# Removing the 22 filler products of TensorE from the first sequence of a fused mLSTM and ternary-FFN kernel

## The chip, the cores and the metric

The kernel runs on one core of one Trainium2 chip. The metric is device time in microseconds (us) of one execution; several executions are timed and the median is given. One execution is also recorded by the hardware profiler, and all rows below come from that one.

## The reference, cut to what matters

The input x has 16 independent sequences of 512 tokens by 512 features, in float32. Each goes through an mLSTM block and a feed-forward block, both with a layer norm ahead and a residual behind:

```python
x = x + mlstm(layernorm(x), Wq, Wk, Wv, Wog, Wig, big, Wfg, bfg, gamma, Wout)
w1_q, w2_q = ternary(w1), ternary(w2)        # sign(w) where |w| >= 0.7 * mean|w|, else 0
x = x + gelu(layernorm(x) @ w1_q.T + b1) @ w2_q.T + b2
```

The mLSTM has 8 heads and, step by step, a decaying state; the kernel computes it in four chunks of 128 tokens (scores within a chunk, a state between chunks), divides by a norm, normalises each head, multiplies by a sigmoid gate and projects with Wout. The ternary weights w1 (2048 by 512) and w2 (512 by 2048) have to be made from float32 weights once, before the first feed-forward block can start.

## The kernel before, in words

One program works through the 16 sequences. In its order the mLSTM of sequence b lies beside the feed-forward block of sequence b - 1: TensorE's list (the function `sequence` of the tensor block) mixes the products of both. Five engines each have one fixed list of instructions, written out by hand, and meet at semaphores.

The first sequence, b = 0, has no feed-forward block of an earlier sequence beside it. Its `sequence(0, None, True)` instead contains the one-time work on weights. `outer(b)` is followed by `first_heads()` (line 2155), which the change touches. The names needed to follow it:

- `scores(0, g)` (products at line 1913) makes the scores of four heads; VectorE multiplies them by the decay (`weigh`, line 1426), and GpSimd zeroes what lies in the future (`earlier_only`, line 661).
- `chunk_heads(j)` makes the output of chunk j, 8 heads, with the float32 products of line 1950 (two records each, so 16 per chunk); at j = 1 it first issues the 48 small products of line 1939 with the states of the chunks before.
- `head_stats` on VectorE (lines 1446 to 1514) reads the result of a chunk and computes its norms. It is followed on VectorE by the other chunks' `head_stats`, in order.
- `ternary_transpose(q)` (line 1789) is 8 transposes of 128 by 128 in float16, of pair q of blocks of w1 or w2, into bank q % 2 of the PSUM tile `pf`. It waits for `small_gone(q)` on VectorE (line 1213), which divides the weights by the threshold, and for `ternary_out(q - 2)` on ScalarE (line 832), which takes the sign and so frees the bank.
- `weights_out` transposes Wout (line 1756, float32); ScalarE and VectorE split it into two float16 parts (`weights_hi`, line 793; `weights_lo`, line 1192). `weights_ready(*USES_OUT)` waits for the last of these splits, and `project(0, t)` (12 products, line 1871) needs them.
- `keep_busy(bank, times)` is the filler: it issues `times` products of 128x128 by 128x512 in float16 (identity times a piece of `wT`) into a bank of `pf`. Nobody reads their result; a transpose overwrites the bank. `busy_until(q, times)` waits until bank q % 2 is free, issues the filler there and then calls `ternary_transpose(q)`.

In `first_heads()` the filler stands at three places: 6 products ahead of `ternary_transpose(5)`, 8 ahead of `ternary_transpose(9)`, and 8 in bank 0 ahead of `weights_ready(*USES_OUT)` and the first projection. TensorE's clock is granted at one of two levels, and the profile shows the granted share: 1.00 is 2.4 GHz and 0.50 is 1.2 GHz.

Of the kernel before, what the change touches and what calls it, by code (L numbers as in the profile page):

```python
# [46 lines left out]
HI, LO = 0, 1  # L47
# [24 lines left out]
def block_program(nc, x, Wq, Wk, Wv, Wog, Wig, big, Wfg, bfg, gamma, Wout, w1, b1, w2, b2, out):  # L72
    B, S, D = x.shape
# [47 lines left out]
    with ExitStack() as ctx:  # L121
        def sb(name, shape, dt=F32):
            return ctx.enter_context(nc.sbuf_tensor(name, shape, dt))

        def pb(name):
            return ctx.enter_context(nc.psum_tensor(name, [P, 2, 512], F32))

        def sem(name):
            return ctx.enter_context(nc.semaphore(name))


        wT = sb("wT", [P, 2, KD, 4 * D], F16)
# [8 lines left out]
        ident16 = sb("ident16", [P, P], F16)  # L141
# [70 lines left out]
        pa, pf = pb("pa"), pb("pf")  # L212
# [42 lines left out]
        pf_free = [sem("pf_free0"), sem("pf_free1")]  # L255
# [99 lines left out]
        def tok(t):  # L355
            return slice(t * P, (t + 1) * P)
# [78 lines left out]
        def pair_halves(q):  # L435

            return (x2T[:, :, :, :, :].rearrange("p a t k c -> p (a t k c)")
                    .rearrange("p (n u d) -> p n u d", n=4, u=2)[:, q % 4, :, :])

        def pair_bank(q):  # L440
            return pf[:, q % 2, :].bitcast(F16).rearrange("p (u k c) -> p u k c", u=2, c=P)
# [1296 lines left out]
        def _(pe):  # L1738
# [39 lines left out]
            def weights_ready(*uses):  # L1778
                for n in uses:
                    pe.wait_ge(s_wfree[w_bank(n)], w_taken(n) + 1)  # L1780

            def ternary_transpose(q):

                pe.wait_ge(s_small_gone, q + 1)
                if q >= 2:
                    pe.wait_ge(pf_free[q % 2], q // 2)
                for i in range(2):
                    for k in range(KD):
                        last = nc.tensor.transpose(pair_bank(q)[:, i, k, :], pair_halves(q)[:, i, tok(k)], ident16[:, :])
                last.then_inc(s_ufill, 1)  # L1790

            def keep_busy(bank, times):

                for _ in range(times):
                    nc.tensor.matmul(bank, ident16[:, :], wT[:, HI, 0, 0:D], start=True, stop=True)

            def take_pa(b, use):

                count = pa_taken(b, use)
                if not (isinstance(count, int) and count == 0):  # L1800
                    pe.wait_ge(pa_free[pa_bank(b, use)], count)
                return pa[:, pa_bank(b, use), :]
# [21 lines left out]
            def x_ready(b):  # L1824

                if b == 0:
                    for n in range(2):
                        pe.wait_ge(pa_free[n], KD // 2)
                elif b == 1:
                    pe.wait_ge(x1T_loaded, 32)  # L1830
                else:
                    pe.wait_ge(xT_loaded, at(b, 16, -16))

            def gates(b):
                bank = take_pa(b, U_GATE)
                for n, (ws, xs) in enumerate(PARTS):
                    for k in range(KD):
                        last = nc.tensor.matmul(bank[k * QUAD:(k + 1) * QUAD, :], wgT[:, k, ws, :], xT[:, xs, :, k, :],  # L1838
                                                start=(n == 0), stop=(n == 2), skip_group_check=True)
                last.then_inc(pa_fill, 1)  # L1840
# [10 lines left out]
            def tokens(b, use, src, col):  # L1851

                token_products(take_pa(b, use), src, col).then_inc(pa_fill, 1)

            def late_values(b, t):

                if not (isinstance(b, int) and b == 0):
                    pe.wait_ge(ph_free, at(b, PH_USES, 0))
                if t == 1:
                    if not (isinstance(b, int) and b == 0):  # L1860
                        pe.wait_ge(ps_free[1], at(b, PS_USES[1], 0))
                    bank, fill = ps[:, 1, :], ps_fill
                else:
                    bank, fill = ph[:, t - 2, :], ph_fill
                token_products(bank, xT[:, :, t, :, :], C_V).then_inc(fill, 1)
# [33 lines left out]
            def scores(b, g):  # L1899

                heads_of = range(g * H4, (g + 1) * H4)
                for n in heads_of:
                    if not in_ps(n):
                        take_pa(b, score_use(n))
                    elif n > 0 or not (isinstance(b, int) and b == 0):
                        pe.wait_ge(ps_free[n % 2], ps_done(b, n) - 1)
                if g == 0:
                    pe.wait_ge(kq_split, at(b, 2, 2))
                for j in range(T):
                    for i, (ks, qs) in enumerate(PARTS):  # L1910
                        for h, n in enumerate(heads_of):
                            rows_of = slice(h * DQ, (h + 1) * DQ)
                            last = nc.tensor.matmul(score_bank(n)[:, tok(j)], k_halves[rows_of, ks, g, tok(j)],  # L1913
                                                    q_halves[rows_of, qs, g, tok(j)], start=(i == 0), stop=(i == 2))
                            if j == T - 1 and i == 2 and h > 0:
                                last.then_inc(ps_fill if in_ps(n) else pa_fill, 1)
# [48 lines left out]
            def project(b, t):  # L1965
                pe.wait_ge(hoT_loaded[t], at(b, 16, 16))
                tokens(b, U_Y + t, hoT[:, t, :, :, :], C_OUT)
# [60 lines left out]
            def sequence(b, fb, ahead):  # L2028
# [63 lines left out]
                if first:  # L2092
                    first_heads()
                    return
# [39 lines left out]
                late_values(b, 1)  # L2134
                tokens(b, U_V, xT[:, :, 0, :, :], C_V)

            def busy_until(q, times):

                pe.wait_ge(pf_free[q % 2], q // 2)
                keep_busy(pf[:, q % 2, :], times)  # L2140
                ternary_transpose(q)

            def chunk_heads(j):

                chunk_state(0, j)
                for h in range(NH):
                    chunk_head(0, j, h)

            def weights_out(*ks):

                for k in ks:
                    pe.wait_ge(pa_free[k % 2], pa_done(0, U_H0 + k % 2))
                weights(*(USES_OUT[k] for k in ks))

            def first_heads():

                scores(0, 0)
                ternary_transpose(2)
                ternary_transpose(3)
                scores(0, 1)  # L2160
                ternary_transpose(4)
                busy_until(5, 6)
                chunk_heads(0)
                ternary_transpose(6)
                chunk_heads(1)
                ternary_transpose(7)
                weights_out(0, 1)
                chunk_heads(2)
                chunk_heads(3)
                ternary_transpose(8)  # L2170
                weights_out(2, 3)
                busy_until(9, 8)
                pe.wait_ge(pf_free[0], 5)
                keep_busy(pf[:, 0, :], 8)
                weights_ready(*USES_OUT)
                project(0, 0)
                ternary_transpose(10)
                ternary_transpose(11)
                project(0, 1)
                ternary_transpose(12)  # L2180
                ternary_transpose(13)
                ternary_transpose(14)
                x_ready(1)
                gates(1)
                ternary_transpose(15)
                late_values(1, 1)
                tokens(1, U_V, xT[:, :, 0, :, :], C_V)
                project(0, 2)
                project(0, 3)
# [44 lines left out]
```

## Time and profile before

| what | value |
|---|---|
| median of 3 executions | 1758.36 us (1758.11 to 1758.88) |
| the profiled execution: its own time | 1758.34 us |
| the profiled execution: span from first to last instruction | 1756.6 us |
| mean granted clock of TensorE | 0.992 |
| TensorE (PE) busy | 1710.4 us, 97% |
| VectorE (DVE) busy | 1445.4 us, 82% |
| ScalarE (ACT) busy | 1051.5 us, 60% |
| GpSimd (POOL) busy | 606.7 us, 35% |

All times in rows count from the span's start. PE stands for TensorE's products, PEld for its loads of the stationary operand, SP for the queue of the DMA issues. A row of a timeline merges neighbouring instructions of one kind: its length runs from the first one's start to the last one's end. In brackets stands how long the engine had been idle and what released it. The chain of work that ended last is followed back from the last instruction to whatever released each step.

### The profile page before, as it was taken

Reading aid. Unit: us, or ns where it says so; the run is one execution under the profiler, and the core shown is the slowest. Engines: PE = TensorE matmul, PEld = TensorE weight load, DVE = VectorE, ACT = ScalarE, POOL = GpSimd, SP = SyncE. Lnnn points to the kernel's source line nnn. Section 1 sums busy time; section 2 is a strip of 40 time slices with the busy share of each in tenths; the row PEclk is TensorE's granted clock in tenths of the full one; section 3 lists DMA queues with packets and bytes.
Section 4 is the critical chain, followed back from the end, with each engine's and each line's share of the span. In section 5 each row is a group of like instructions: output and inputs, shape, how many; then the busy total and the mean of one; then the engine's idle time right before and its main releaser. Section 6 shows DMA issues by size and latency. Waiting matters only on the chain.

```text
span 1756.6 us, 31370 instructions
## 1 busy us (share of the span) xinstructions
PE 1710.4 (97%) x12026; PEld 842.8 (48%) x12026; DVE 1445.4 (82%) x2536; ACT 1051.5 (60%) x1761; POOL 606.7 (35%) x477
## 2 busy tenths in 40 slices
PE   5789999999999999999999999999999999999999
PEld 3454444444454444445444444444445444454455
DVE  6778979888897978889887897988789797886872
ACT  5857557383764837466483755738376483746643
POOL 1142423525143352414425242342514335241440
PEclk8899999999999999999999999999999999999999
DMA  8736243272534526253362724426253452624120
GB/s 294 216 95 158 59 126 97 55 176 60 133 83 104 130 55 167 59 128 86 90 153 53 163 59 121 103 55 177 60 137 78 100 135 55 142 63 131 33 55 25
DMA packets 294981, 187.45 MB, mean 107 GB/s; under 512 B 239136, under 2 KB 260640, under 8 KB 289712
## 3 DMA queue, kind: packets, MB, share of 16 engines
q1 hardware_dynamic: 293248, 182.30, 40.9%
q10 hardware_dynamic: 1584, 3.15, 0.5%
q8 instruction: 95, 1.56, 0.4%
q14 instruction: 54, 0.44, 0.1%
HBM read 96.47 MB, written 20.23 MB: 66 GB/s over the span
## 4 chain that ended last, share of the span: by engine, by line
PE 85%; DVE 8%; DMA 2%; issue 2%; SPq 1%; ACT 1%; POOL 1%; POOLq 0%; DVEq 0%; ACTq 0%
PE pf L2018 24%; PE pf L2002 22%; PE pa L1871 19%; PE pa L1847 7%; PE psh L1871 6%; PE psh L1958 2%; SPq L530 1%; DMA kT<-shared 1%; PE psh L1913 1%; PE psh L1992 1%; PE pa L1838 1%; PE pa L1958 1%; PE psh L1954 1%; DVE gT L1577 1%; PE psh L1894 1%
## 5 line engine op out<-in xcount | busy, mean ns | idle before, releaser
L2018 PE MATMUL pf<-w2T,gT 128*128 128x512 f16 x2048 | 505.9, 379 | 0.0
L2002 PE MATMUL pf<-x2T,w1T 128*128 128x512 f16 x1920 | 422.0, 379 | 0.0
L2002 PEld LDWEIGHTS pf<-x2T,w1T 128*128 128x128 f16 x1920 | 185.3, 98 | 222.7
L2018 PEld LDWEIGHTS pf<-w2T,gT 128*128 128x128 f16 x2048 | 195.4, 97 | 177.5 <-DVE ktok L1456 0.5
L1577 DVE SCALAR_TENSOR_TENSOR gT<-g,wscale,gT 128x512 f16<-128x512 f32 x240 | 209.8, 878 | 20.2 <-ACT gT L986 18.1
L1871 PE MATMUL pa<-wT,xT 128*128 128x512 f16 x960 | 213.0, 379 | 1.9 <-ACT sig L910 1.9
L983 ACT ACTIVATE g<-pf,b1c 128x512 f32<-128x512 f32 x240 | 164.0, 683 | 72.5 <-PE pf L2002 58.0
L1871 PE MATMUL pa<-wT,shared 128*128 128x512 f16 x768 | 177.5, 381 | 4.5 <-DVE wT L1192 3.7
L986 ACT ACTIVATE gT<-g,wscale 128x512 f16<-128x512 f32 x240 | 173.3, 722 | 7.8
L1847 PE MATMUL pa<-xT,wT 128*128 128x512 f16 x768 | 171.8, 380 | 0.9 <-ACT kT L928 0.8
L991 ACT ACTIVATE ktok<-kT 128x512 f32<-128x512 f32 x64 | 40.4, 631 | 217.5 <-DVE kT L1472 217.5
L950 ACT ACTIVATE dec<-dec,gtok 128x128 f32<-128x128 f32 x512 | 154.5, 394 | 0.0
L1871 PEld LDWEIGHTS pa<-wT,xT 128*128 128x128 f16 x960 | 94.0, 98 | 114.7 <-ACT sig L910 2.0
L679 POOL TENSOR_TENSOR dec<-dec 128x1024 f16<-128x1024 f32 x30 | 72.0, 2398 | 200.1 <-ACT dec L1001 200.1
L1871 PE MATMUL psh<-wT,xT 128*128 128x512 f16 x576 | 129.5, 379 | 0.0
L700 POOL TENSOR_TENSOR x1b<-xres,b2r 128x512 f32<-128x512 f32 x64 | 80.6, 1268 | 132.6 <-DVE xres L1534 128.9
L684 POOL TENSOR_TENSOR hinv<-hvar,half 128x8 f32<-128x8 f32 x64 | 105.2, 1644 | 49.8 <-DVE hvar L1514 49.8
L1871 PEld LDWEIGHTS pa<-wT,shared 128*128 128x128 f16 x768 | 75.0, 98 | 96.7 <-DVE wT L1192 4.2
L691 POOL TENSOR_TENSOR qT<-kT,qT 128x512 f16<-128x512 f32 x64 | 74.4, 1163 | 132.7 <-ACT qT L1010 132.7
L661 POOL TENSOR_SCALAR_AFFINE_SELECT dec<-dec 128x1024 f32<-128x1024 f32 x64 | 92.1, 1439 | 72.4 <-DVE dec L1426 72.2
L1847 PEld LDWEIGHTS pa<-xT,wT 128*128 128x128 f16 x768 | 74.6, 98 | 87.9 <-ACT kT L928 0.9
L651 POOL TENSOR_TENSOR rstd<-ve,half 128x4 f32<-128x4 f32 x16 | 16.1, 1008 | 277.9 <-DVE ve L1238 277.9
(243 smaller groups left out, 2704.4 us busy)
## 6 DMA issues: line engine op xcount, KB each, us to landing
dec<-gate_r SPq DMA_DIRECT2D x32, 1024.0 KB, 5.8
xin<-L_attn_x SPq DMA_DIRECT2D x16, 1024.0 KB, 6.0
out<-x1b SPq DMA_DIRECT2D x64, 256.0 KB, 2.2
xres<-L_attn_x SPq DMA_DIRECT2D x16, 512.0 KB, 4.1
xres<-L_attn_x SPq DMA_DIRECT2D x32, 256.0 KB, 3.0
qw<-gate_w SPq DMA_DIRECT2D x128, 48.0 KB, 2.0
s<-state_w SPq DMA_DIRECT2D x60, 97.5 KB, 2.3
qw<-kT SPq DMA_DIRECT2D x120, 48.0 KB, 2.0
```

The lines of the kernel that those rows point to most:

```text
L661: nc.gpsimd.affine_select(out=rows_of, in_=rows_of, compare_op=ALU.is_ge, fill=0.0, base=0, pattern=[[0, 2 * T], [1, P]], channel_multipli ...
L684: nc.gpsimd.tensor_tensor(hinv[:, :], hvar[:, :], half[:, :], ALU.pow).then_inc(pool_a, 1)
L691: nc.gpsimd.tensor_tensor(head_parts[j % 2][:, LO, :], cent[j % 2], head_parts[j % 2][:, HI, :], ALU.subtract).then_inc(ho_lo[j], 1)
L700: nc.gpsimd.tensor_tensor(x1b[:, t, :], xres[:, t, :], b2r[:, :], ALU.add).then_inc(x1b_ok, 1)
L950: last = nc.scalar.activation(dec[:, h, tok(j)], dec[:, h, tok(j)], ACT.Exp, bias=gtok[:, j, ROW_C, h:h + 1])
L983: nc.scalar.activation(g32[:, f % 2, :], pf[:, use % 2, :], ACT.Gelu, bias=b1c[:, f:f + 1], scale=1.0 / X_SCALE).then_inc(pf_free[use % 2], 1)
L986: nc.scalar.activation(gT[:, HI, f, :], g32[:, f % 2, :], ACT.Copy, scale=wscale[:, W_GELU:W_GELU + 1]).then_inc(g_hi, 1)
L1577: nc.vector.scalar_tensor_tensor(gT[:, LO, f, :], g32[:, f % 2, :], wscale[:, W_GELU:W_GELU + 1], gT[:, HI, f, :], ALU.mult, ALU.subtract) ...
L1847: last = nc.tensor.matmul(bank, wT[:, ws, k, col:col + P], xT[:, xs, :, k, :], start=(k == 0 and n == 0), stop=(k == KD - 1 and n == 2))
L1871: last = nc.tensor.matmul(bank, src[:, xs, k, :], wT[:, ws, k, col:col + D], start=(k == 0 and n == 0), stop=(k == KD - 1 and n == 2))
L2002: last = nc.tensor.matmul(bank, w1T[:, k, tok(f)], x2T[:, part, :, k, :], start=(k == 0 and part == HI), stop=(k == KD - 1 and part == LO))
L2018: last = nc.tensor.matmul(bank, gT[:, part, f, tok(t)], w2T[:, f, :], start=(f == 0 and part == HI), stop=(f == NF - 1 and part == LO), sk ...
```

## The change

It deletes `keep_busy` and `busy_until` and their three uses. The transposes for pairs 5 and 9 are called directly. Nothing is added; the order of everything else stays.

```diff
-            def keep_busy(bank, times):
-
-                for _ in range(times):
-                    nc.tensor.matmul(bank, ident16[:, :], wT[:, HI, 0, 0:D], start=True, stop=True)
...
-            def busy_until(q, times):
-
-                pe.wait_ge(pf_free[q % 2], q // 2)
-                keep_busy(pf[:, q % 2, :], times)
-                ternary_transpose(q)
-
...
                 ternary_transpose(4)
-                busy_until(5, 6)
+                ternary_transpose(5)
                 chunk_heads(0)
...
                 weights_out(2, 3)
-                busy_until(9, 8)
-                pe.wait_ge(pf_free[0], 5)
-                keep_busy(pf[:, 0, :], 8)
+                ternary_transpose(9)
                 weights_ready(*USES_OUT)
                 project(0, 0)
```

## Rows read from the trace of the kernel before

**Rows 1.** The page: share of the span by engine in the chain that ended last

```profile
PE 85%; DVE 8%; DMA 2%; issue 2%; SPq 1%; ACT 1%; POOL 1%; POOLq 0%; DVEq 0%; ACTq 0%
```

**Rows 2.** The chain that ended last, 60 to 135 us: start us, length us, engine, tile, line

```profile
85.58 1.49 POOL dec L661
...
87.20 1.99 PE pa L1950 x16
...
89.21 0.44 DVE ktok L1446
...
93.60 0.71 DVE ktok L1456
...
111.24 0.75 DVE wT L1192
```

**Rows 3.** All instructions of line 1795: duration ns min/median/max, first and last start

```profile
L1795 PE MATMUL pf<-wT,ident x22: 379/380/634, 83.7 to 108.3; 128*128 128x512 f16 x22
```

**Rows 4.** The timeline of PE: start us, length us, [idle before, releaser]

```profile
16.46 1.97 PE L1821 MATMUL pa<-ident,xin 128*128 128x128 f32 x8 [1.56 <-DVE xT L1250]
...
46.63 1.97 PE L1756 MATMUL pf<-ident,gT 128*128 128x128 f32 x8 [8.11 <-DVE wT L1192]
...
49.51 3.19 PE L1847 MATMUL pa<-xT,wT 128*128 128x512 f16 x12
...
83.69 1.90 PE L1795 MATMUL pf<-wT,ident 128*128 128x512 f16 x6
...
86.17 0.62 PE L1789 MATMUL pf<-ident,x2T 128*128 128x128 f16 x8 [0.57 <-DVE x2T L1213]
...
91.05 2.00 PE L1950 MATMUL psh<-vaug,dec 128*128 128x65 f32 x16
...
93.33 1.04 PE L1756 MATMUL pa<-ident,x1b 128*128 128x128 f32 x8
...
102.71 3.05 PE L1795 MATMUL pf<-wT,ident 128*128 128x512 f16 x8
...
106.29 0.62 PE L1789 MATMUL pf<-ident,x2T 128*128 128x128 f16 x8 [0.53 <-DVE x2T L1213]
...
106.75 1.89 PE L1795 MATMUL pf<-wT,ident 128*128 128x512 f16 x8
...
112.35 4.19 PE L1871 MATMUL pa<-wT,shared 128*128 128x512 f16 x12 [3.71 <-DVE wT L1192]
...
121.67 0.61 PE L1789 MATMUL pf<-ident,x2T 128*128 128x128 f16 x8 [0.76 <-ACT w2T L832]
```

**Rows 5.** Busy time by stretch: PE, PEld, DVE, ACT, POOL, granted clock, DMA, GB/s

```profile
18.00:19.00 1.00, 0.43 (x3) 0.03 (x1) 0.68 (x1) 0.74 (x3) 0.00 (x0) 0.50 1.02 92
...
47.00:48.00 1.00, 1.00 (x7) 0.99 (x6) 0.89 (x2) 0.23 (x2) 0.00 (x0) 0.50 0.89 360
...
50.00:51.00 1.00, 1.00 (x5) 0.39 (x4) 1.00 (x3) 1.00 (x2) 0.00 (x0) 0.78 0.98 410
...
81.50:84.40 2.90, 2.90 (x58) 2.30 (x59) 1.92 (x4) 0.46 (x1) 1.45 (x2) 0.50 0.91 304
...
84.70:87.20 2.50, 1.51 (x13) 0.67 (x11) 2.50 (x4) 0.64 (x2) 2.25 (x2) 1.00 0.32 61
...
108.70:111.80 3.10, 0.00 (x0) 0.00 (x0) 3.00 (x7) 0.63 (x1) 1.34 (x3) 1.00 0.00 0
...
112.30:115.20 2.90, 2.85 (x7) 1.02 (x8) 1.70 (x4) 0.00 (x0) 2.10 (x2) 0.50 0.47 90
...
115.40:121.60 6.20, 5.52 (x50) 3.34 (x47) 5.91 (x8) 3.49 (x5) 3.54 (x3) 1.00 0.34 85
...
160.00:1756.60 1596.60, 1589.42 (x11165) 772.26 (x11163) 1322.95 (x2284) 946.48 (x1581) 570.18 (x434) 1.00 0.40 98
```

**Rows 6.** The timeline of DVE: start us, length us, count

```profile
85.37 2.24 DVE L1213 TENSOR_SCALAR x2T<-gT,w 128x1024 f16<-128x1024 f32 x2
...
118.09 1.89 DVE L1213 TENSOR_SCALAR x2T<-gT,w 128x1024 f16<-128x1024 f32 x2
```

## The prediction, made before the changed kernel was run

> **What bounds the kernel now.** I read the page's chain first: 85% of the span is TensorE [rows 1]. From 160 us to the end PE is busy for 1589.4 of 1596.6 us at a granted clock of 1.00 [rows 5]. So what the first sequence loses, the end loses too, unless it falls into a wait. Next I read the chain piece by piece around the filler [rows 2]. There the chain is seldom on PE: it goes through GpSimd's masking (85.58), through PE's chunk 0 (87.20, 1.99 us), then through VectorE from 89.21 to the last split of Wout at 111.24, and returns to PE with the first projection at 112.35. Then the listing of line 1795 and PE's timeline [rows 3, 4] give the fillers and what follows each, and the table of stretches gives the clock [rows 5].
>
> **The direct part: taking out 22 products.** There are 22, at 379 ns as the median record [rows 3]; as stretches they are 6 in 1.90 us, 8 in 3.05 us and 8 in 1.89 us, together 6.84 us of busy PE [rows 4]. None is on the chain. After the first stretch PE still sat idle for 0.57 us until VectorE had divided pair 5; after the second 0.53 us until it had divided pair 9; after the third 3.71 us until Wout was split [rows 4]. Taken out, the same waits are 6.84 us longer in sum and end at the same times. Direct gain: 0. The waits on `pf_free` that go with the filler cost nothing either, since the filler started ahead of these slacks. No DMA and no other queue is touched.
>
> **The indirect part: the clock.** The granted clock is 0.50 over 81.50 to 84.40 and 1.00 over 84.70 to 87.20. The first filler began at 83.69 inside the cold stretch, so in the 2.9 us before 84.40 the engine was busy throughout, but only for 2.2 us of it (81.50 to 83.69) with other work [rows 4, 5]. With the filler gone PE works for some 2.4 us, then waits until 86.17, does 8 transposes, waits again and begins chunk 0 at 87.20. Does the clock still rise before chunk 0? Two rows lie on either side. The burst of 1.97 us at 16.46 left the clock at 0.50 a little later, in 18 to 19 us [rows 4, 5]. The burst from 112.35 was at 0.50 for 2.85 us of work and stood at 1.00 from 115.40 [rows 5]. The 2.4 us lie between, nearer to the burst that failed, and with a wait behind it; I take it that the clock stays at 0.50 and that chunk 0 runs cold.
>
> The Trainium skill, page "TensorE: Matmul & The Clock Gate", section on PE-mode transpose, says that transposes do not count as busy work for the clock. By that rule the remaining burst holds even less that counts and the sum would be the forecast's, 1761.0. The trace does not quite agree: the clock rose within 50 to 51 us (mean 0.78) when most of the busy time behind it, from 46.63 to 49.5, was float32 transposes and only 1 us or so products [rows 4, 5]. If transposes do count, the burst may suffice, and the time is the first rival's, 1758.4.
>
> *Price of chunk 0 cold.* No row has these products at 0.50. The nearest float32 work at both levels is 8 transposes: 1.97 us cold (46.63; clock 0.50 in 47 to 48) against 1.04 us warm (93.33), a factor 1.89 [rows 4, 5]. 1.99 us x 0.89 = 1.8 us. The lower bound is 0 (the clock rises in time), the upper a full doubling, 2.0 us. It lies on the chain: VectorE's copy at 89.21 waits for it [rows 2], and everything VectorE does from there to 111.24 stands behind. So +1.8 us.
>
> *Chunk 1.* PE ended it at 91.05 + 2.00 = 93.05, VectorE took it at 93.60, 0.55 us later [rows 2, 4]. Both sides move by 1.8 us. If the clock is back soon after chunk 0, nothing is added: 0. If it is not, chunk 1 adds 2.00 x 0.89 = 1.8 less 0.55, so up to 1.2 us, and more if the products of line 1939 are cold too. I take 0, since PE is busy without a pause from 87.20 and the burst from 112.35 regained the clock in about 3 us.
>
> *Second and third filler.* They kept the clock up to some time before 112.3, but not long enough: over 108.70 to 111.80 PE did nothing, and the first projection began at 0.50 in the kernel before too, 12 products in 4.19 us with the clock back by 115.40 [rows 4, 5]. Without them it starts cold just the same. Only the moment at which the clock comes back may move, as the projection now begins 1.8 us later. Cold over its whole length it would take 12 x 2.85 / 7 = 4.9 us (7 products in 2.85 us [rows 5]), with the last one's tail 5.1 us: +0.9 us over 4.19. Bounds: 0 if the clock needs as long as before; if it stays down over the second projection too, 0.9 plus another 12 x (0.41 - 0.22) = 2.3 us (0.22 is 1.89 / 8 less the tail, [rows 4]), so 3.2 us, less the wait of 0.76 us at 121.67 [rows 4], some 2.4 us. I take +0.9, as the start no longer falls where it did.
>
> Pair 9's transposes cold (0.62 us becomes about 1.0) delay ScalarE by 0.4 us, which the long wait for Wout hides; without it they would cost these 0.4 us.
>
> **Sum.** 0 + 1.8 + 0 + 0.9 = +2.7 us. The profiled execution took 1758.34 us (its span 1756.6 and 1.7 around it), 0.02 from the median, so no correction: **1761.0 us**, +0.15%. Its own range: 1760.1 (1.8, and the second term 0) to 1762.7 (2.0 + 2.4). A measurement of this kernel can tell a difference of about 0.2% (3.5 us) from none, so the forecast counts as no change.
>
> **Rivals.**
> - *The clock comes up anyway* (transposes and scores are enough): chunk 0 runs warm, the projection starts as before at 112.35. Every filler was then useless: 1758.4 us. For it: the rise at 50 us, and that 2.4 us is not far from 2.85. Against: the burst at 16.46.
> - *The clock stays down long, and the time is measurably worse.* In the stretch from 87.20 the float32 products are short, and if they do not bring the clock back until chunk 1 is over, the price is 1.8 + at least 1.2, with line 1939's 1.57 us of small products also cold some 3 us in all for the middle, and 2.4 more at the projections: 1.8 + 1.2 + 0.5 + 2.4 = 5.9, 1764.2 us. It decides from the point where the clock is still 0.50 at the start of chunk 1, about 93 us. For it: the chunk is preceded by two waits, and the projection by a very long one. Against: 2.85 us sufficed at 112.35.
> - *The fillers slowed VectorE*, by reading SBUF beside it. The divisions at 85.37 took 2.24 us for two; at 118.09, with no filler, 1.89 [rows 6]. Were the 0.35 us and the like at pair 9 due to the filler, and the clock of no consequence, the kernel would gain under 1 us: 1757.6. Against: the difference is small, and other engines work there as well.
> - That the change does not do what it says can be left out: the diff leaves no call of the filler.
>
> **How the numbers follow.** Forecast 0.55, clock comes up anyway 0.22, clock stays down long 0.18, VectorE relieved 0.05. The range goes from 1758.0, which holds the first rival, to 1763.0, which holds the forecast's upper bound; left out are most of the third case and the fourth. Slower by over 0.2% (above 1761.9): the long-cold case and some 0.08 of the forecast's upper part, 0.26. Faster by over 0.2%: no case reaches it, 0.03. The rest, 0.71, is within.
>
> **What the profile would show.** Right: line 1795 gone; PE's waits before 86.17, 106.3 and 112.4 longer by the fillers' lengths; the granted clock 0.50 over 84.7 to 89 us and 16 products of chunk 0 in some 3.8 us; VectorE's second copy at 91.0 and the projection at about 114.2 with 5.1 us for its 12 products; from there every row later by 2.7. Wrong: chunk 0 in 2.0 us (first rival), chunk 1 in much over 2 us or both projections cold (second), shorter divisions on VectorE (third).

## The result and the profile after

The changed kernel takes 1763.71 us in the median of 7 executions (1763.17 to 1766.12), the kernel before, on the same chip in 7 executions, 1758.24 us. The ratio is 1.0033, with a 95% interval from 1.0022 to 1.0044: slower by 5.5 us in the medians. The forecast was 1761.0 us with a range to 1763.0. The profiled execution took 1763.17 us, its span 1761.4 us, which is 4.8 us more than the span of before; the accounts below compare these two executions.

PE's timeline of the changed kernel comes first, in the columns of [rows 4]. The line numbers behind the deleted functions are smaller by 5 and more: 1945 is the old 1950 (chunk products), 1934 the old 1939, 1866 the old 1871.

```profile
82.52 1.03 PE L1789 MATMUL pf<-ident,x2T 128*128 128x128 f16 x8
...
85.83 1.04 PE L1789 MATMUL pf<-ident,x2T 128*128 128x128 f16 x8 [2.27 <-DVE x2T L1213]
...
86.86 3.65 PE L1945 MATMUL pa<-vaug,dec 128*128 128x65 f32 x16
...
91.29 2.84 PE L1934 MATMUL psh<-cst,qw 32*128 32x65 f32 x48
...
94.06 3.67 PE L1945 MATMUL psh<-vaug,dec 128*128 128x65 f32 x16
...
98.39 1.91 PE L1756 MATMUL pa<-ident,x1b 128*128 128x128 f32 x8
...
100.09 4.15 PE L1945 MATMUL psh<-vaug,dec 128*128 128x65 f32 x32
...
111.18 0.95 PE L1789 MATMUL pf<-ident,x2T 128*128 128x128 f16 x8 [4.19 <-DVE x2T L1213]
...
117.23 4.87 PE L1866 MATMUL pa<-wT,shared 128*128 128x512 f16 x12 [5.10 <-DVE wT L1192]
...
127.23 0.61 PE L1789 MATMUL pf<-ident,x2T 128*128 128x128 f16 x8 [0.76 <-ACT w2T L832]
```

The table of stretches, in the columns of [rows 5]:

```profile
83.70:85.80 2.10, 0.00 (x0) 0.00 (x0) 2.10 (x5) 0.91 (x1) 1.66 (x2) 0.50 0.82 317
...
86.90:90.50 3.60, 3.60 (x18) 3.60 (x19) 0.79 (x2) 3.57 (x3) 0.00 (x0) 0.50 0.71 275
...
90.60:100.90 10.30, 10.30 (x93) 9.99 (x90) 6.91 (x20) 4.25 (x6) 2.68 (x2) 0.50 0.49 178
...
111.90:117.20 5.30, 0.23 (x3) 0.00 (x0) 5.13 (x11) 2.17 (x3) 3.47 (x4) 0.50 0.25 47
...
117.30:121.60 4.30, 4.30 (x11) 1.51 (x12) 2.92 (x5) 0.63 (x1) 2.76 (x3) 0.51 0.32 61
```

Chunk 0's 16 products are at 86.86 and take 3.65 us, where they took 1.99 [rows 2]. Chunk 1's, at 94.06, take 3.67 instead of 2.00 [rows 4], and the 48 small products ahead of them 2.84. The granted clock is 0.50 over 86.90 to 90.50 and over 90.60 to 100.90, although PE is busy for all of these 3.6 and 10.3 us. It comes back behind 100.9. Then a long wait follows, the clock is down again by 111.9, and the first projection runs at 0.50 (12 products in 4.87 us; before 4.19).

These rows answer to 89.21, 93.60 and 111.24 of [rows 2]. The first two are from VectorE's timeline, and the last fence is from the chain that ended last:

```profile
90.55 0.43 DVE L1446 COPY ktok<-pa 128x260 f32<-128x260 f32 x1 [1.28 <-PE pa L1945]
...
97.84 0.70 DVE L1456 COPY ktok<-psh 128x520 f32<-128x520 f32 x1 [2.94 <-PE psh L1945]
```

```profile
98.59 1.72 PE pa L1756 x8
...
116.13 0.75 DVE wT L1192
```

The sums: just before chunk 0 this execution was 0.34 us ahead of the one before (pair 5's transposes at 85.83 against 86.17 [rows 4]). Counted from there, VectorE's second copy is 90.55 - 89.21 + 0.34 = 1.7 us late, the copy of chunk 1 is 97.84 - 93.60 + 0.34 = 4.6 us late and Wout's last split 116.13 - 111.24 + 0.34 = 5.2 us late. So chunk 0 costs 1.7 us, chunk 1 with its small products 2.9 us more, and 0.6 us are added between chunk 1 and Wout. A part of these 0.6 may be Wout's transposes, which took 1.91 us at 98.39 instead of 1.04 (93.33 [rows 4]): the chain now runs through them (98.59), and before it did not. No run separates this part. The projection adds 4.87 - 4.19 = 0.7. PE's transposes that stood at 121.67 [rows 4] stand at 127.23, 5.6 us later, and the end is later by only 4.8. Of this difference of 0.8, 0.7 lies in PE's waits in later sequences for the scores that VectorE multiplies by the decay, in these two rows of the table of waits of PE (who waited for whom, us in total, times, longest). First the kernel before, from 122 us to the end:

```profile
PE psh L1913 <- DVE dec L1426: 1.2, 3, 0.6
```

and the kernel after, from 118 us to the end:

```profile
PE psh L1908 <- DVE dec L1426: 0.5, 2, 0.3
```

### The profile page after: what moved, and what is told of

Read it like the earlier page. It is cut to its first block, busy times and chain, and to the rows that moved or that the text cites. A ratio compares the mean times of both kernels' runs of the same rounds, so it can differ in the third digit from the quotient of the medians.

```text
span 1761.4 us, 31326 instructions
## 1 busy us (share of the span) xinstructions
PE 1710.8 (97%) x12004; PEld 846.6 (48%) x12004; DVE 1445.5 (82%) x2536; ACT 1051.5 (60%) x1761; POOL 607.7 (34%) x477
## 4 chain that ended last, share of the span: by engine, by line
PE 88%; DVE 6%; DMA 2%; issue 1%; SPq 1%; ACT 1%; POOL 1%; POOLq 0%; DVEq 0%; ACTq 0%
PE pf L2013 24%; PE pf L1997 23%; PE pa L1866 19%; PE pa L1842 8%; PE psh L1866 6%; PE psh L1953 2%; PE psh L1908 1%; PE psh L1987 1%; SPq L530 1%; PE pa L1833 1%; DMA kT<-shared 1%; PE pa L1953 1%; PE psh L1889 1%; PE psh L1949 1%; DMA gT<-L_attn_Wv 0%
```

## The experiments

The theory after the result was: only the clock is at work, the first filler is the one that matters, and the chunk products do not bring the clock back once it is down. The rivals: the later fillers carry part of the loss; and it is only the time for which PE is busy that counts, not what it does. Every run is compared with the kernel before on its own chip, and medians are given. The ratio beside them is estimated from all executions and is not the quotient of the two medians. "Dense products" are the filler's own, of 512 columns in float16.

**Only the first filler out.**

```diff
-                busy_until(5, 6)
+                ternary_transpose(5)
```

> Only the first filler (6 products ahead of pair 5) is out; the second and third stay. Theory A (the loss is that chunks 0 and 1 run at 0.50 because nothing brings the clock back before them): the whole middle loss is here. Chunk 0's 16 products take about 3.65 us instead of 1.99, line 1939's 48 products 2.8 instead of 1.57, chunk 1's 3.65 instead of 2.00, and the last split of Wout is about 4.9 us later than before: 1762.6 to 1763.7 us. Theory B (the fillers share the loss, the second and third carrying some half of it through the projection): about 1760.5 us.

Measured: 1763.71 us against 1758.72, ratio 1.0026 (1.0017 to 1.0035). That is 5.0 of the 5.5 us, the whole loss within the intervals, and the later fillers, which are still in, save nothing that can be seen. The profiled execution was one of the longest of its kernel (1765.6 us). In its timeline chunk 0 is at 88.01, chunks 2 and 3 at 101.23 and the projection at 120.32:

```profile
86.97 1.03 PE L1789 MATMUL pf<-ident,x2T 128*128 128x128 f16 x8 [2.26 <-DVE x2T L1213]
...
88.01 3.64 PE L1950 MATMUL pa<-vaug,dec 128*128 128x65 f32 x16
...
99.53 1.91 PE L1756 MATMUL pa<-ident,x1b 128*128 128x128 f32 x8
...
101.23 6.92 PE L1950 MATMUL psh<-vaug,dec 128*128 128x65 f32 x32
...
108.81 1.72 PE L1756 MATMUL pa<-ident,x1b 128*128 128x128 f32 x8
...
120.32 4.44 PE L1871 MATMUL pa<-wT,shared 128*128 128x512 f16 x12 [3.74 <-DVE wT L1192]
```

and in its stretches the clock stands at 0.50 for 26.2 us, in which PE is busy for 23.9:

```profile
83.70:109.90 26.20, 23.94 (x169) 23.12 (x167) 17.65 (x36) 11.07 (x12) 9.70 (x8) 0.50 0.47 158
```

The 2.26 us that are missing are the wait ahead of 86.97; from there to 109.90 PE worked without a gap. Even chunks 2 and 3 were at 0.50 here (32 products in 6.92 us); in the changed kernel's profile they were mostly at 1.00 (4.15 us, at 100.09). That is the kind of difference that spreads the executions of these kernels over 3 to 4 us.

**Only the second and third filler out.**

```diff
-                busy_until(9, 8)
-                pe.wait_ge(pf_free[0], 5)
-                keep_busy(pf[:, 0, :], 8)
+                ternary_transpose(9)
```

> The first filler stays, the second and third (16 products) are out. Theory A: chunks 0 and 1 are warm as before, PE's waits are longer, and only the clock at the first projection can move, 4.2 us before against at most 5.1: 1758.2 to 1759.1 us. Theory B: about 1760.5 us. Pair 9's transposes may take 1.0 instead of 0.62 us without effect.

Measured: 1758.64 us against 1758.72, ratio 0.9998 (0.9989 to 1.0006). These 16 products saved nothing. Timeline and stretches:

```profile
83.99 2.38 PE L1795 MATMUL pf<-wT,ident 128*128 128x512 f16 x6
...
87.49 1.97 PE L1950 MATMUL pa<-vaug,dec 128*128 128x65 f32 x16 [0.42 <-POOL dec L661]
...
112.63 4.68 PE L1871 MATMUL pa<-wT,shared 128*128 128x512 f16 x12 [5.01 <-DVE wT L1192]
```

```profile
86.00:98.40 12.40, 11.90 (x146) 10.88 (x144) 10.74 (x24) 8.62 (x10) 4.02 (x3) 1.00 0.60 212
...
100.00:112.60 12.60, 3.77 (x24) 3.11 (x25) 12.18 (x26) 5.50 (x8) 8.80 (x8) 0.50 0.26 42
...
112.70:116.40 3.70, 3.70 (x9) 1.21 (x10) 2.50 (x5) 0.63 (x1) 2.15 (x3) 0.50 0.37 71
```

Chunk 0 takes 1.97 us, and the clock is 1.00 over 86.00 to 98.40. It is 0.50 over the whole of 100.00 to 112.60, but there PE does 3.8 us of work off the path. The projection takes 4.68 us. So each part of the change done alone gives a clear answer: the first filler 5.0 us, the other two 0.

**The first filler replaced by short float32 products.** The next two runs and the one after ask what kind of work does it. The computation stays whole in all of them; only what is written into the free bank changes. In all three the second and third filler are out as well, which the diffs shown leave out, so the run just above is the one to compare them with.

```diff
-                busy_until(5, 6)
+                pe.wait_ge(pf_free[1], 2)
+                for _ in range(4):
+                    nc.tensor.matmul(pf[:, 1, 0:VA], ident[:, :], vaug[:, 0, 0, :], start=True, stop=True)
+                ternary_transpose(5)
```

> The second and third filler are out; the first is replaced by 4 float32 products of 128x128 by 128x65 (8 records, some 1.8 us at 0.50), the same form as the chunk products, so the engine is busy for about as long as with the 6 filler products. Theory K (the kind of work decides: these products do not bring the clock back, as chunks 0 and 1 did not in 12 us of unbroken work): the clock is 0.50 at 87 us, chunk 0 takes 3.65 us and the time is 1763 to 1764 us. Theory T (it is the time for which the engine is busy): chunk 0 takes 2.0 us and the time is that of the kernel without the later fillers, 1758.2 to 1759.1 us.

Measured: 1763.59 us against 1758.72, ratio 1.0028 (1.0017 to 1.0039), and all 7 executions at 1762.7 or above. The replacement is the row at 84.35:

```profile
84.35 1.92 PE L2164 MATMUL pf<-vaug,ident 128*128 128x65 f32 x8
...
87.86 3.65 PE L1950 MATMUL pa<-vaug,dec 128*128 128x65 f32 x16
```

```profile
83.70:86.30 2.60, 2.56 (x16) 2.37 (x14) 2.60 (x5) 1.02 (x1) 1.66 (x3) 0.50 1.07 324
...
86.30:100.40 14.10, 13.58 (x109) 13.03 (x110) 7.98 (x17) 6.54 (x6) 4.09 (x3) 0.50 0.56 199
```

PE is busy for 2.56 of the 2.6 us up to 86.30, as with the products, and for 13.6 of the 14.1 us after it, and the clock stays at 0.50. So the time for which the engine is busy does not alone decide whether the clock comes back.

**The first filler replaced by 16 float16 transposes.**

```diff
-                busy_until(5, 6)
+                pe.wait_ge(pf_free[1], 2)
+                for n in range(16):
+                    nc.tensor.transpose(pair_bank(5)[:, n // 4 % 2, n % 4, :], ident16[:, :], ident16[:, :])
+                ternary_transpose(5)
```

> The second and third filler are out; the first is replaced by 16 float16 transposes of 128 by 128 (some 1.7 us at 0.50), again about the busy time of the 6 products, with dense 128-column work. If transposes do not count for the clock (the Trainium skill, page TensorE: Matmul & The Clock Gate, section on PE-mode transpose, says so), chunk 0 is at 0.50 and takes 3.65 us: 1763 to 1764 us. If they count like products, chunk 0 takes 2.0 us: 1758.2 to 1759.1 us. From the trace of before alone, where the clock rose at 50.4 us behind mostly float32 transposes, the second is somewhat likelier.

Measured: 1763.04 us against 1758.72, ratio 1.0019 (1.0010 to 1.0028), so the expectation that the second outcome was likelier missed. But the 11 executions are not of one kind: three lie at 1758.79, 1758.80 and 1760.12 us, the other eight between 1761.9 and 1764.1. The three have a mean granted clock of 0.989, the eight one of 0.985 to 0.987. The profiled one is of the longer sort (chunk 0 in 3.65 us), so no profile shows a short one:

```profile
83.85 1.91 PE L2164 MATMUL pf<-ident 128*128 128x128 f16 x16
...
87.36 3.65 PE L1950 MATMUL pa<-vaug,dec 128*128 128x65 f32 x16
```

**The first filler replaced by 8 float32 transposes** (same place and bank, `nc.tensor.transpose(pf[:, 1, tok(n % 4)], ident[:, :], ident[:, :])`, 8 times).

> The later fillers are out; the first is replaced by 8 float32 transposes of 128 by 128 (1.9 us at 0.50), as long as 16 float16 transposes or 8 short float32 products. Theory W (float32 transposes, 128 columns wide, do bring the clock back, as at 50.4 us in the kernel before and at 101 us in the changed one, both just behind such transposes): chunk 0 takes 2.0 us and the time is 1758.2 to 1759.1 us. Theory N (no transpose brings it back, the products around them did): chunk 0 takes 3.65 us and the time is 1763 to 1764 us. The 16 float16 transposes came out mostly on the slow side, so N is not excluded; I expect most executions at 1759.

Measured: 1761.84 us against 1758.26, ratio 1.0019 (1.0009 to 1.0030), with executions from 1758.2 to 1765.4 us, of which three of 8 lie at 1760.6 or below. Neither theory has it, and "most executions at 1759" missed. The profiled execution shows how that comes:

```profile
83.48 1.33 PE L2164 MATMUL pf<-ident 128*128 128x128 f32 x8
...
86.99 3.21 PE L1950 MATMUL pa<-vaug,dec 128*128 128x65 f32 x16 [0.42 <-POOL dec L661]
```

The 8 transposes took 1.33 us, against 1.97 for 8 wholly at 0.50 [rows 4], so the clock rose among them. It did so early: the granted clock is 0.50 over 83.50 to 84.00 and 0.94 over 84.00 to 84.50, so the rise came about 0.6 us behind their start, and the scores ahead of them may have a share in it. Chunk 0 then took 3.21 us: the clock fell again while chunk 0 ran. In this execution it was not the rise that was missing, but what would have held the clock.

**The first filler with 3 products instead of 6**, the later ones out.

```diff
-                busy_until(5, 6)
+                busy_until(5, 3)
```

> Only the first filler, with 3 products instead of 6. If the clock wants the whole stretch from the scores to the end of the filler filled, 3 products are mostly not enough and the executions fall into two groups, some at 1758.5 us (chunk 0 at 1.00), the rest at 1762 to 1764 us. If any dense products suffice, all lie at 1758.5 us.

Measured: 1762.80 us against 1757.89, ratio 1.0029 (1.0018 to 1.0041), all 7 executions at 1761.3 or above. Neither of the expected outcomes came: there is no second group at 1758.5. Timeline, and PE's busy time and granted clock in short stretches:

```profile
83.69 1.33 PE L1795 MATMUL pf<-wT,ident 128*128 128x512 f16 x3
...
86.16 0.62 PE L1789 MATMUL pf<-ident,x2T 128*128 128x128 f16 x8 [1.14 <-DVE x2T L1213]
...
87.20 2.78 PE L1950 MATMUL pa<-vaug,dec 128*128 128x65 f32 x16 [0.42 <-POOL dec L661]
...
93.53 3.67 PE L1950 MATMUL psh<-vaug,dec 128*128 128x65 f32 x16
```

```profile
84.50:85.00 0.50, 0.50 (x2) 0.77 1.09 369
...
85.00:87.50 2.50, 0.94 (x12) 1.00 0.51 147
...
87.50:88.00 0.50, 0.50 (x7) 1.00 0.33 131
...
88.00:88.50 0.50, 0.50 (x6) 0.65 0.85 360
```

Here it can be seen directly. The clock rises within 84.50 to 85.00, behind the second and third product; in the 2.5 us up to 87.50 PE works for only 0.94 us, most of it 8 transposes; and the clock falls within 88.00 to 88.50, with chunk 0 under way. Chunk 0 takes 2.78 us and chunk 1, at 93.53, the full 3.67. In the kernel before, with the same times up to here (83.69, 86.17, 87.20 [rows 4]), chunk 0 kept the clock. So in this execution the last three products of the filler were not needed to raise the clock but to keep it.

**A longer third filler.** The kernel before wasted its second and third filler: the wait for Wout was longer than they lasted, and the projection began at 0.50 all the same. Three of the next four runs make it longer.

```diff
-                keep_busy(pf[:, 0, :], 8)
+                keep_busy(pf[:, 0, :], 20)
```

> The kernel before with 20 instead of 8 products in the third filler, so that PE works until some 1 us before Wout's last split. Theory: the first projection then starts at 1.00 and takes 2.75 instead of 4.2 us, PE's next stage is PE's own, so 1.4 us less than before: about 1757.3 us. Rival: VectorE is busy with divisions until 116.5 us anyway and the projection's result waits for it, so nothing is won: 1758.7 us.

Measured: 1756.88 us against 1758.26, ratio 0.9993 with an interval from 0.9984 to 1.0002. The size is the expected one; the interval alone would still allow no gain. The timeline shows the mechanism:

```profile
106.61 4.48 PE L1795 MATMUL pf<-wT,ident 128*128 128x512 f16 x20
...
112.21 2.75 PE L1871 MATMUL pa<-wT,shared 128*128 128x512 f16 x12 [1.12 <-DVE wT L1192]
...
120.10 0.61 PE L1789 MATMUL pf<-ident,x2T 128*128 128x128 f16 x8 [0.76 <-ACT w2T L832]
```

The filler lasts until 111.1, the projection begins at 112.21 at full clock and takes 2.75 us, and the transposes of 121.67 [rows 4] stand at 120.10, earlier by 1.6; 0.1 of it this execution was ahead before the filler (106.61 against 106.75).

**The same without the second filler**, the third with 16 products.

```diff
-                busy_until(9, 8)
+                ternary_transpose(9)
...
-                keep_busy(pf[:, 0, :], 8)
+                keep_busy(pf[:, 0, :], 16)
```

> First filler as before, second out, third with 16 products in place of 8. Without the second the clock is 0.50 when the third begins (about 107.6 us), so the 16 take some 5 us and end about when Wout's last split does, with the clock up by then: the first projection at 1.00 in 2.75 us, the time that of the kernel with 20 products in the third, about 1757 us. Rival: the clock comes back so late that the filler runs past Wout's split and delays the projection: 1758.3 us or above.

Measured: 1756.49 us (1755.95 to 1757.55) against 1757.89, ratio 0.9993 (0.9984 to 1.0002). Again 1.4 us less, again the interval just reaches 1, and all 11 executions lie below the median of the kernel before. The filler ends at 112.5, about when Wout's last split is done, and the projection takes 2.75 us:

```profile
107.50 4.99 PE L1795 MATMUL pf<-wT,ident 128*128 128x512 f16 x16
...
112.73 2.75 PE L1871 MATMUL pa<-wT,shared 128*128 128x512 f16 x12 [0.23 <-issue]
...
120.61 0.61 PE L1789 MATMUL pf<-ident,x2T 128*128 128x128 f16 x8 [0.76 <-ACT w2T L832]
```

**Five products ahead of the second scores.**

```diff
                 ternary_transpose(3)
+                pe.wait_ge(pf_free[0], 2)
+                keep_busy(pf[:, 0, :], 5)
                 scores(0, 1)
```

> The kernel before with 5 more filler products, in the wait ahead of scores(0, 1), once ScalarE has freed bank 0. If they hold the clock at 1.00 (they begin about 2.5 us after the last products that ran at 1.00), the scores of the second four heads take 0.85 instead of 1.46 us, on the chain: 0.6 us less than before, 1758.1 us where before gives 1758.7. If the clock falls all the same, nothing changes, or they delay the scores by some 0.3 us.

Measured: 1758.63 us against 1758.26, ratio 1.0006 (0.9997 to 1.0014): no gain, and executions up to 1763.0 us, where the kernel before has none above 1759.5 on that chip.

```profile
80.49 1.55 PE L1795 MATMUL pf<-wT,ident 128*128 128x512 f16 x5 [0.21 <-ACT w1T L832]
...
112.85 5.28 PE L1871 MATMUL pa<-wT,shared 128*128 128x512 f16 x12 [3.71 <-DVE wT L1192]
```

The five products took 1.55 us (eight took 1.89 at full clock [rows 4]), so the clock fell among them; they delayed the scores by some 0.3 us, and the scores ran at 0.50 as before. The projection, with the third filler of the old length, is at 0.50 for its whole 5.28 us in this execution: here even dense products, without a gap, did not bring the clock back in that time.

**Both additions** (the last diff and the 20 products).

> Both additions together: 5 products ahead of scores(0, 1) and 20 in the third filler. If each does what its own run is expected to do, 0.6 + 1.4 = 2.0 us less than before, about 1756.7 us; the gains are in different stages, so they should add.

Measured: 1756.53 us against 1758.26, ratio 0.9990 (0.9981 to 0.9999). The gain is 1.7 us where 2.0 were expected. It is the only version whose interval lies wholly below 1, but it is not clearly better than the longer third filler alone (1756.88, on the same chip), and the early products gain nothing by themselves. So the gain is put down to the third filler, which all three versions with 1.4 to 1.7 us less have in common.

## Why the prediction was wrong

Point by point, by its own steps:

- *Direct part, 0.* Right. PE's waits at 85.83, 111.18 and 117.23 still end on VectorE, and taking out the second and third filler alone changes nothing.
- *The clock stays down before chunk 0.* Right, in the profile (0.50 over 83.70 to 85.80) and in the run with only the first filler out.
- *Price of chunk 0, +1.8 us.* Right: 3.65 instead of 1.99 us, and 1.7 us on VectorE's copy.
- *Chunk 1: "I take 0, since PE is busy without a pause from 87.20 and the burst from 112.35 regained the clock in about 3 us".* **This is the step that failed.** The clock stayed at 0.50 for 14 us of unbroken work, and chunk 1 with its small products cost 2.9 us, as much as the rest of the gap between forecast and result. The two bursts were taken for the same thing because both keep PE busy. The one from 112.35 consists of products of 512 columns in float16; the one from 87.20 of float32 products of 65 columns, products on 32 rows and float16 transposes. The run with short float32 products in the filler's place shows that the first of these kinds, for as long as the 6 dense products, did not bring the clock back in any of 7 executions. Which property decides, the width or the type, no run separates.
- *Upper bound of chunk 1, "up to 1.2 us, and more if the products of line 1939 are cold too".* The "more" was left without a number here and entered the second rival as 0.5 us, too low: from the end of chunk 0 to the end of chunk 1 PE took 97.73 - 90.51 = 7.2 us instead of 93.05 - 89.19 = 3.9, since the transposes and the 48 small products (2.84 us, 1.27 more than before) between the chunks were at 0.50 too; less the 0.55 us that VectorE had in hand that is 2.8.
- *Projection, +0.9 us.* About right, 0.7. The moment at which the clock comes back moves from execution to execution: the same 12 products took 4.68 us with the second and third filler out and 5.28 in the run with five products more.
- *Every loss is the end's loss.* Nearly: 0.8 us of 5.6 were won back later, 0.7 of them in waits of PE for VectorE. The 0.6 us between chunk 1 and Wout stand in no term of the sum.
- *The rule of the Trainium skill* (page "TensorE: Matmul & The Clock Gate", section on PE-mode transpose, by which transposes do not count as busy work): the runs agree in part. With 16 float16 transposes 8 of 11 executions lost the clock, by their times and mean clocks, and 3 did not, where without any filler there none of 18 kept it; with 8 float32 transposes the clock rose in the profiled execution, and in the changed kernel it rose behind such transposes too (98.39). So the rule looks too strict for this kernel. It would not have saved the forecast: it says nothing on short float32 products, which fill most of the time from 87.20.

What came true is the second rival, "the clock stays down long", with its point of decision (0.50 at 93 us) and its mechanism; its price of 5.9 us stands against 4.8 in the profile and 5.5 in the medians. That the price is so near is in part luck: it has 1.7 us for chunk 1 and its small products, which cost 2.9, and 2.4 for the projections, which cost 0.7, since the second one ran at full clock (12 products at 122.83 in 2.75 us). It had a chance of 0.18. The range ended at 1763.0 because most of that rival was left out of it. That the fillers slowed VectorE can be dropped: the divisions of pairs 5 and 6 took 2.24 us [rows 6] in the changed kernel as well, in a row at 85.02.

Still open: why the clock rose at 101 us in the changed kernel's profile and not in the run with the first filler out, where it rose only at 110. Float32 transposes of Wout stand ahead of both rises, and the same holds in all six profiles in which the clock was 0.50 at chunk 1: it came back 1.1 to 3.1 us behind the start of a group of 8 of them. In four it was the first group (98.39 in the changed kernel); in the runs with the first filler out and with 3 products the first group (99.53 and 97.86) brought nothing and the second (108.81 and 107.14) stood ahead of the rise. No run separated the transposes from what lies around them.

## What to carry to other kernels

A filler is to be judged by the stretch of weak work behind it: here 6 dense products kept the clock for some 12 us of mostly short float32 work, which did not regain it in 14 us and more of its own, and were worth 5 us, while 16 products whose wait outlasted them were worth nothing. Before taking a burst as one that will bring the clock back, look at what it is made of, and find a row in which the same kind of work did so. Where a filler stands in a wait, make it last until the wait ends or shortly before: the same place gave 1.4 us with 16 or 20 products, with intervals that just reach no gain, and 0 with 8.

## What the runs showed of the hardware

- Work that fills PE without a gap, or nearly so, can leave the clock at 0.50: 13.6 us of 14.1 in the run with short float32 products, and all of the time from 86.97 to 109.90 with the first filler out.
- The clock can fall while PE is busy: with 3 products it fell within 88.00 to 88.50, with chunk 0 under way since 87.20, and in the run with float32 transposes chunk 0 lost it too.
- The same program takes one side or the other from execution to execution when the filler is marginal: 1758.8 to 1764.1 us with 16 float16 transposes, against 1757.4 to 1759.3 us in the 11 executions with the 6 dense products alone.
